# A four-step graph network kernel: type sums in short instructions, extra rows moved ahead, messages before scans

## The reference

```
def step(feat, _):
    transformed = jnp.einsum('nd,khd->knh', feat, W) + b[:, None, :]   # 4 edge types
    msgs = transformed[etypes, src]
    a = jax.ops.segment_sum(msgs, dst, num_segments=num_nodes)
    feat = _gru_cell(a, feat, w_ih, w_hh, b_ih, b_hh)
...
seg_sum = jax.ops.segment_sum(edge_attr, row, num_segments=N)
seg_max = jax.ops.segment_max(edge_attr, row, num_segments=N)
```

## Time and profile before

| | us |
|---|---|
| median of 3 runs | 7,605.77 (7,584.76 to 7,704.37) |
| the profiled execution | 7,588.8, span 7,587.1 |
| PE busy | 4,931.1 (65%) |
| VectorE, ScalarE, GpSimd busy | 4,188.5, 4,037.2, 3,838.4 |
| step 0, first product to end of contraction | 1,036.8 to 3,053.2 |
| step 1, first product | 3,102.4 |
| end of step 3's contraction, about | 5,890 |

### The profile page before, as it was taken

The page is one execution under the profiler, slowest core; times in us unless marked ns, Lnnn a source line. Parts: engine busy times, 40 slices in busy tenths (PEclk is TensorE's granted clock), DMA queues, the critical chain, the costliest instruction groups (busy, mean ns, idle before and its releaser), DMA issues. The chain is left out here.

```text
span 7587.1 us, 95171 instructions
## 1 busy us (share of the span) xinstructions
PE 4931.1 (65%) x39275; PEld 2509.5 (33%) x39275; DVE 4188.5 (55%) x6700; ACT 4037.2 (53%) x3030; POOL 3838.4 (51%) x3297
## 2 busy tenths in 40 slices
PE   0120135655544443899998999889999467666678
PEld 0110123332222221455554555545555311111123
DVE  9889953333322222455544555445554499999700
ACT  0000048888655654566664666646656177777501
POOL 0027778888877771577772677726771000000130
PEclk9955567877777776999998999999999666676799
DMA  9920035555433337466664776646666143333398
GB/s 414 429 41 0 0 115 200 199 196 198 150 134 139 140 139 134 160 229 235 207 219 139 232 242 214 213 143 229 237 217 203 36 163 149 153 153 153 130 417 361
DMA packets 344776, 1414.97 MB, mean 186 GB/s; under 512 B 129310, under 2 KB 182836, under 8 KB 314516
## 3 DMA queue, kind: packets, MB, share of 16 engines
q1 hardware_dynamic: 159676, 1138.67, 40.8%
q10 hardware_dynamic: 79672, 239.96, 8.8%
q0 software_dynamic: 104992, 30.24, 3.2%
HBM read 1008.21 MB, written 400.36 MB: 186 GB/s over the span
## 5 line engine op out<-in xcount | busy, mean ns | idle before, releaser
L556 PE MATMUL ps_all<-ring,T 128*64 128x448 f16 x32928 | 3323.2, 364 | 1069.9 <-ACT ring L713 1051.2
L556 PEld LDWEIGHTS ps_all<-ring,T 128*64 128x64 bf16 x32928 | 1902.7, 113 | 2472.2 <-ACT ring L713 789.8
L407 POOL DMA_INDIRECT mat_d<-cT,idxT x1563 | 1866.6, 1194 | 965.5 <-ACT cT L654 489.7
L451 POOL DMA_INDIRECT R<-in_edge_attr,eid x1568 | 1793.4, 1144 | 694.4 <-issue 477.2
L712 ACT ACTIVATE ring<-ring 128x3136 uint16<-128x3136 uint8 x504 | 1415.3, 2808 | 1330.2 <-DVE t L1047 823.5
L713 ACT ACTIVATE ring<-ring 128x3136 uint16<-128x3136 uint8 x504 | 1411.4, 2800 | 0.0
L1071 DVE TENSOR_TENSOR R<-ring 128x6272 uint16<-128x6272 uint16 x49 | 168.2, 3433 | 1363.5 <-ACT ring L713 1363.5
L1624 POOL DMA_INDIRECT sg<-seg_d,endI x49 | 56.9, 1161 | 1206.6 <-POOLq L178 1192.0
L510 PE MATMUL ps_all<-ident,R 128*128 128x128 f32 x448 | 109.7, 426 | 807.1 <-DVE R L807 807.1
L1567 PE MATMUL ps_all<-ad,ones 3*128 3x384 bf16 (+1 forms) x686 | 322.5, 470 | 337.1 <-ACT ps_all L1537 336.2
L1036 DVE TENSOR_SCALAR ring<-ring 128x3136 uint16<-128x3136 uint16 x308 | 303.7, 986 | 390.4 <-PE ps_all L556 265.0
(11 more groups left out here) (373 smaller groups left out, 3913.1 us busy)
## 6 DMA issues: line engine op xcount, KB each, us to landing
ring<-mat_d SPq DMA_DIRECT2D x784, 784.0 KB
C<-csum_d SPq DMA_DIRECT2D x98, 3136.0 KB, 15.3
mat_d<-ring SPq DMA_DIRECT2D x98, 1568.0 KB, 39.7
csum_d<-R ACTq DMA_DIRECT2D x196, 784.0 KB, 3.7
seg_d<-R ACTq DMA_DIRECT2D x32, 1568.0 KB
msg_d<-t ACTq DMA_DIRECT2D x196, 128.0 KB
R<-in_edge_attr,eid POOLq DMA_INDIRECT x1568
mat_d<-cT,idxT POOLq DMA_INDIRECT x1563
```

What stands on the lines that cost most here:

```text
L407: pool.indirect_dma_start(mat_d, bass.IndirectOffsetOnAxis(idxT[:, col:col + 1], 0), cT[:, col:col + 1], None).then_inc(s_sc[g % 8], 16)
L451: pool.indirect_dma_start(slab[n % 2][:, c, 0:FA], None, attr, bass.IndirectOffsetOnAxis(eid[:, at:at + 1], 0)).then_inc(s_at[n % 2], 16)
L556: mm = pe.matmul(accs[h * D:(h + 1) * D, j, 0:GW], lhsT, ring[:, n % 6, h * HQ + j * GW:h * HQ + (j + 1) * GW], start=first, stop=True, sk ...
```

## The change

It does four things. (1) `added` sums in 16 instructions instead of 3: two rounds of four uint16 adds over quarters, then eight `scalar_tensor_tensor` of 784 elements that add the fourth piece, write fp32 into the store buffers and give row sums; ScalarE only issues the stores. (2) All 49 messages of step 0 are made and stored once before step 0 (`early`), by products into PSUM banks 0 and 1; step 0 makes them again for its own use. (3) The extra rows' scatters and the gathers of their messages stand inside the stream of scatters, behind the 673rd, and their pieces are contracted before step 0's last block (`walk`); pieces from the extra rows on are widened by both engines. (4) In steps 1 to 3 VectorE makes the message and widens before it scans; a slab is scanned in three blocks instead of four, and GpSimd gathers the extra rows' messages ahead of a slab's gathers.

```diff
+EXTRA_GROUP = 42
+EXTRA_BLOCK = 42
...
+def walk(st):
+    return list(range(BPS)) if st else [*range(NB - 1), NB, NB + 1, NB - 1]
...
-        who = "act" if n < KT * NB or n % 2 else "dve"
+        who = "act" if n < KT * (NB - 1) or n % 2 else "dve"
...
+            psE = [bank(k)[:, 0:KT * D] for k in range(2)]
+            sumW = QW // 2
...
+                    if k == EXTRA_GROUP * GC:
+                        extra_placed()
+                        gathered(0)
...
-                pool.wait_ge(s_xs, 16 * NSG)
...
+                    if n and n % PER == 0 and n // PER < STEPS - 1:
+                        gathered(n // PER)
                     for c in range(SLAB):
                         at = n * SLAB + c
                         pool.indirect_dma_start(slab[n % 2][:, c, 0:FA], None, attr,
                                                 bass.IndirectOffsetOnAxis(eid[:, at:at + 1], 0)).then_inc(s_at[n % 2], 16)
-                    if n and n % PER == 0 and n // PER < STEPS - 1:
-                        gathered(n // PER)
...
+                for c in range(NB):
+                    if c >= 2:
+                        pe.wait_ge(s_tc, c - 1)
+                    product(c, psE[c % 2])
+                pe.wait_ge(s_tc, NB)
...
                     for o in range(NQ):
-                        n = c * NQ + o
-                        if n >= 2:
-                            act.wait_ge(s_cso[o % 2], 16 * (n // 2))
-                        act.activation(CS[o % 2], all4[:, o * QW:(o + 1) * QW], ACT.Copy,
-                                       accum_out=rs[:, c % 2, o:o + 1]).then_inc(s_cse, 1)
-                        act.wait_ge(s_cse, n + 1)
+                        act.wait_ge(s_csm, c * NQ + o + 1)
                         act.dma_start(csum[c * P:(c + 1) * P, o * QW:(o + 1) * QW], CS[o % 2]).then_inc(s_cso[o % 2], 16)
...
+                for c in range(NB):
+                    msgs_out(0, c)
                 for st in range(STEPS):
...
+                    for q in quarters:
+                        ad = dve.tensor_tensor(all4[:, q], four[0][:, q], four[1][:, q], ALU.add)
+                    link(ad)
+                    widened(dve, piece_no(0, c, 2))
+                    for q in quarters:
+                        ad = dve.tensor_tensor(all4[:, q], all4[:, q], four[2][:, q], ALU.add)
+                    link(ad)
+                    widened(dve, piece_no(0, c, 3))
+                    for o in range(NQ):
+                        n = c * NQ + o
+                        if n >= 2:
+                            dve.wait_ge(s_cso[o % 2], 16 * (n // 2))
+                        for h in range(2):
+                            at = slice(o * QW + h * sumW, o * QW + (h + 1) * sumW)
+                            ad = dve.scalar_tensor_tensor(CS[o % 2][:, h * sumW:(h + 1) * sumW], all4[:, at], 1.0, four[3][:, at],
+                                                          ALU.mult, ALU.add, accum_out=rs[:, 2 * o + h:2 * o + h + 1])
+                        ad.then_inc(s_csm, 1)
+                    dve.wait_ge(s_csm, (c + 1) * NQ)
+                    dve.tensor_reduce(cn_src[:, c:c + 1], rs[:, :], AX.X, ALU.add).then_inc(s_csr, 1)
...
-                    for f in range(q * FA // 4, (q + 1) * FA // 4):
+                    for f in range(q * FA // 3, (q + 1) * FA // 3):
...
-                        upto(piece_no(st, c, 0) + 5)
-                        if slab_of(st, c) is not None:
-                            scanned(*slab_of(st, c))
+                        upto(min(piece_no(st, c, 0) + 5, end))
                         if c + 2 < NB:
                             message(st, c + 2)
-                        elif c + 1 == NB:
+                        if c == (NB - 1 if st else EXTRA_BLOCK):
                             message_extra(st)
-                        upto(piece_no(st, c, 0) + 7)
...
+                        upto(min(piece_no(st, c, 0) + 7, end))
+                        if slab_of(st, c) is not None and slab_of(st, c)[1] < 3:
+                            scanned(*slab_of(st, c))
```

More of the change, by code:

```diff
@@ L68, with first_pieces, piece_no @@
 assert NS * SLAB == EC and HQ == NG * GW and NQ * QW == NP and SPEC * P + D == HQ and KT < NX <= 2 * KT
-def piece_no(st, c, k):
-    return PPS * st + KT * c + k
 def pieces(c):
     return KT if c <= NB else NX - KT
+def walk(st):
+    return list(range(BPS)) if st else [*range(NB - 1), NB, NB + 1, NB - 1]
+def first_pieces():
+    found = []
+    for st in range(STEPS):
+        n = PPS * st
+        for c in walk(st):
+            found.append(((st, c), n))
+            n += pieces(c)
+    return dict(found)
+FIRST_OF = first_pieces()
+def piece_no(st, c, k):
+    return FIRST_OF[st, c] + k
 def widened_by():
@@ L479, in _ @@
                 for st in range(STEPS):
-                    for c in range(BPS):
+                    for c in walk(st):
                         if st == 0 and c < NB:
@@ L605, in _ @@
                         pe.wait_ge(s_h, NG * st)
-                    product(st, 0)
-                    pe.wait_ge(s_tc, NB * st + 1)
-                    product(st, 1)
-                    for c in range(NB):
-                        contract(st, c)
-                    for c in range(NB, BPS):
-                        contract_extra(st, c)
+                    product(0, psT)
+                    pe.wait_ge(s_tc, NB * (st + 1) + 1)
+                    product(1, psT)
+                    for c in walk(st):
+                        if c < NB:
+                            contract(st, c)
+                        else:
+                            contract_extra(st, c)
                     gates(st)
@@ L759, in grown @@
                         act.activation(nn[j % 2], tt[j % 2], ACT.Tanh, bias=gb[:, 2:3]).then_inc(s_tn, 1)
+                for c in range(NB):
+                    msgs_out(0, c)
                 for st in range(STEPS):
+                    end = PPS * (st + 1) - 1
                     upto(piece_no(st, 0, 0))
-                    msgs_out(st, 0)
+                    if st:
+                        msgs_out(st, 0)
                     upto(piece_no(st, 0, KT - 1))
-                    msgs_out(st, 1)
-                    for c in range(NB):
-                        upto(piece_no(st, c, 0) + 5)
-                        if st == 0:
+                    if st:
+                        msgs_out(st, 1)
+                    for c in walk(st):
+                        upto(min(piece_no(st, c, 0) + 5, end))
+                        if st == 0 and c < NB:
                             sums_out(c)
@@ L1067, in added @@
                     four = [ring[:, piece_no(0, c, k) % 6, :].bitcast(U16) for k in range(KT)]
-                    widened(dve, piece_no(0, c, KT - 1))
-                    if c:
-                        dve.wait_ge(s_cse, c * NQ)
-                    link(dve.tensor_tensor(all4, four[0], four[1], ALU.add))
-                    link(dve.tensor_tensor(all4, all4, four[2], ALU.add))
-                    dve.tensor_tensor(all4, all4, four[3], ALU.add).then_inc(s_csm, 1)
-                def rows_summed(c):
-                    dve.wait_ge(s_cse, (c + 1) * NQ)
-                    own = rs[:, c % 2, :]
-                    link(dve.tensor_tensor(own[:, 4:6], own[:, 0:2], own[:, 2:4], ALU.add))
-                    dve.tensor_tensor(cn_src[:, c:c + 1], own[:, 4:5], own[:, 5:6], ALU.add).then_inc(s_csr, 1)
+                    quarters = [slice(o * QW, (o + 1) * QW) for o in range(NQ)]
@@ new lines, in added @@
+                    widened(dve, piece_no(0, c, 0))
+                    widened(dve, piece_no(0, c, 1))
+                    for q in quarters:
[6 more added lines that the diff above has]
+                    widened(dve, piece_no(0, c, 3))
@@ L1152, in grown @@
                         after(j)
+                for c in range(NB):
+                    early(c)
                 for st in range(STEPS):
+                    end = PPS * (st + 1) - 1
                     upto(piece_no(st, 0, 0))
```

86 lines of the change are left out of this document (43 added, 43 removed).

## The result

The changed kernel takes 7,344 us (median of four runs, 7,334 to 7,461), the kernel before 7,597 beside it; the ratio is 0.967, with a 95% interval of 0.966 to 0.969. One of the four runs took some 120 us more than the rest, as single runs of most kernels here did, and such runs are left out of all ratios. The forecast was 7,330. Its profiled execution takes 7,338.5 us (span 7,336.8), that of before 7,588.8: 250 less, where the prediction's sum said 268. The sum was nearly right, but two of its terms were not: step 0 gave more than it was to give, and steps 1 to 3 lost time instead of gaining.

What follows compares the result with a forecast made beforehand. Step 0 was taken as bound by GpSimd's scatters and a serial tail, steps 1 to 3 by nearly full PE. −186 − 40 − 42 = −268 on 7,588.8 gave 7,321, stated as 7,330 us; range 7,210 to 7,480.

Steps and rivals of the forecast that it cites:

- Sums in short instructions: Step 0's sums: 4.6 us of scatter time lost a block instead of 7.0, gain 110 us; last scatter at 2,767.
- its period is rounded up to whole VectorE instructions: Step 0's sums: a scatter enters at a boundary, every two instructions, 1.86 us; 8.1 scatters in a block's 15.0 us.
- The upper bound: Step 0's sums: loss grows with time held, 10.2 us a block, a loss of 147; as rival 7,578 us, chance 0.07.
- Extra rows: Step 0: eight scatters and seven gathers behind the 673rd scatter, at 1,456 us, add 19 us to the stream.
- rival 2: Step 0, mid-stream: the extra rows' DMA jam stops GpSimd, 80 us more before the last scatter, 7,410 us; chance 0.12.
- the jam: Step 0: DMA stands some 80 us from about 1,475 for the extra rows; PE loses it and makes it up.
- Early messages: Before step 0: 49 products, 60 us, first piece widened at about 1,103; costs nothing, or 60 to 159 without cover.
- Tail: Step 0's end: contraction ends about 100 us after the last scatter instead of 195, at 2,867, 186 earlier than before.
- Messages' gathers: Steps 1 and 2: gathers ahead of slab 11's 49 remove 40.3 us of PE's waits for T3e.
- Piece waits: Steps 1 to 3: 14 us a step, 42 in all, of PE's 79.5 us waiting for widened pieces go; between 0 and 79.5.
- Rate and number of scans stay: Steps 1 to 3: the new order with messages before scans leaves the scans' rate and number unchanged.
- The new deadline: Steps 1 to 3: behind a late slab, the next thing PE lacks comes 11 us later.

Runs made afterwards that it cites:

- the control: The changed kernel with one assertion on register values taken away; 7,333.8 us, ratio 0.968 to the kernel before.
- d4_act_late: Against the control, 40 unused ScalarE copies (about 60 us) between the early messages' stores and step 0's first widening; 7,359.2 us, ratio 0.9705.
- c1_long_adds: Against the control, the eight quarter adds made two whole uint16 adds again, the eight fp32-writing instructions kept; 7,510.1 us, ratio 0.991.
- d3_gather_behind: Against the control, the seven gathers of the extra rows' messages put behind slab 11's (22's) 49 gathers again; 7,422.1 us, ratio 0.980.
- c7_old_scans_gaps: Against the control, four scan portions ahead of the message, VectorE waiting after each portion's fourth pair; 9,493 us on a troubled chip (kernel before 10,341).

## Why the prediction was right, and where not

**Sums in short instructions.** Taken: 4.6 us lost a block, from the step "its period is rounded up to whole VectorE instructions: two of 0.91 to 0.97, 1.86 us". The period was rounded up to two, 1.77 us, and 7.8 scatters a block are caught (8.1 said). The size was off, as a caught scatter loses 0.44 us on the mean, and others pass free between: 3.46 us a block. (The recorded sum is also a little off: 3.8 scatters fewer at 1.265 us are 4.8 us, not 4.6.) 1.14 × 47 = 54 us, and the control's last scatter is 54 us ahead of the 2,767 predicted. The upper bound (the loss goes with the time held) is refuted by the long adds. A scatter beside an add is held for what is left of it, as the rows show. That adds of 1.23 us don't slow a scatter, as the prediction reads in the earlier trace rows, rests on one that started 0.04 us before its add, and isn't shown. The Trainium skill (SBUF — State Buffer, Who interferes with whom) says, of the modes in which VectorE takes the port pair that it shares with GpSimd, that the other side is blocked for the whole instruction; for the adds the trace agrees (held until 0.8 us after the add's end), but a run of scans and the widenings behind it held gathers far longer than any one instruction, up to 5.6 us.

**Extra rows.** GpSimd was not stopped (rival 2), the jam took some 40 us of PE's time (24 busy in 64) and these were made up, as the tail shows, which is no longer than forecast. The eight were issued from 1,443 on (1,456 said).

**Early messages.** First widening at 1,090 (1,103 said), nothing lost that the profile shows; no run took them away alone, d4_act_late only made the same delay longer.

**Tail.** 89 us instead of 100. The sums' leaving ScalarE, which the prediction put at nothing in itself, is part of it: with the sums of before the tail is 19 us longer. Together with the scatters the contraction ended 267 us earlier (251 in the control), not 186.

**Messages' gathers.** −40 said, −40 came in the waits; put back they cost 88.

**Piece waits.** Here the prediction failed: −42 said, +47 measured. The step that failed is "Rate and number of scans stay". The number stayed; the rate of the gathers did not (a slab every 75 to 79 us instead of 72 to 76), because the prediction priced the order of the scans only by what VectorE does later, and neither the length of their runs nor what now stands directly behind them. The trace of before held gathers of up to 3.18 us beside 16 scans, which could have been put to use: six scans more are 1.3 us more for a gather that is caught, and the two widenings that the new order puts behind the scans are 1.8 more. The new deadline, 11 us later, may have come; but slabs 5 us later each eat it in two slabs. Steps 1 to 3 as a whole were to give 82 us and took 15 more: 89 of the difference are these waits, the rest isn't traced. The two errors, −65 to −81 in step 0 and +97 in the steps, nearly cancel, and that the forecast of 7,330 met 7,344 is in part luck.

## What to carry to other kernels

Where VectorE and GpSimd run side by side, don't count VectorE's busy time but the longest stretch in which GpSimd can't get in: cut long two-input instructions into pieces shorter than GpSimd's own period, and break runs of very short ones by a wait of 0.1 us. A gap that costs VectorE 7 waits a slab gave 145 us here. When a loop is cut into fewer, longer portions, or moved, price the length of the unbroken run, with the instructions that follow it at once, even where number and place of the instructions seem to be all that changes.

## What the runs showed of the hardware

- A run of 16 scans, 0.215 us apart, makes a gather take up to 3.18 us; one of 22 with a wait behind it up to 3.84; one of 20 to 22 with two widenings directly behind it up to 5.6 (6.2 once in the control); at most eight with a gap of 0.12 us behind them up to 2.66, mostly 0.95. The held gather ends 0.8 us after the last instruction of the unbroken run. More than half of the gathers that start within a run of scans aren't held at all; what decides is in part how far into the run they start.
- The same can be much longer. In three of the fourteen profiles, of c1_long_adds, d3_gather_behind and c7_old_scans_gaps (this one on the troubled chip), one scatter beside the second sort stood for 136.9 us, while VectorE issued over 250 instructions one after the other, 0.33 to 0.85 us apart. It ended 0.8 us after VectorE's first pause of 0.11 us. The executions of the first two took 138 and 116 us more than the median of their kernels' runs. First that of c1_long_adds, then the same place in the changed kernel, where the scatters got in:

```profile
569.66 136.88 POOL L447 DMA_INDIRECT mat_d<-cT,idxT  x1 [0.30 <-issue]
570.00 0.59 DVE L848 SCALAR_TENSOR_TENSOR R<-R 128x256 f32<-128x256 f32 x1
```

```profile
573.22 1.24 POOL L447 DMA_INDIRECT mat_d<-cT,idxT  x1 [0.30 <-issue]
573.54 0.60 DVE L849 SCALAR_TENSOR_TENSOR R<-R 128x256 f32<-128x256 f32 x1
```

  Same instructions, same order, and the same phase to some hundredths of a us (the scatter starts 0.18 us into an instruction of VectorE here, 0.20 there); what decides isn't shown. Because of this hold the last scatter of c1_long_adds in its profile (3,014) is not used above.
- A reduction, with its single input, doesn't hold GpSimd, where an instruction with two inputs of the same length does. Timeline of c1_long_adds: beside a reduction of 3,136 elements (3.42 us) the scatters take 0.96, beside the two-input instruction behind it 3.98:

```profile
521.28 3.42 DVE L234 TENSOR_REDUCE m<-ring 128x49 f32<-128x3136 f32 x1 [0.58 <-DVE i_place L1012]
522.92 0.96 POOL L447 DMA_INDIRECT mat_d<-cT,idxT  x1 [0.31 <-issue]
...
525.17 3.43 DVE L236 TENSOR_TENSOR ring<-ring,m 128x3136 f32<-128x3136 f32 x1
525.45 3.98 POOL L447 DMA_INDIRECT mat_d<-cT,idxT  x1 [0.30 <-issue]
```

  The Trainium skill (SBUF — State Buffer, Who interferes with whom) says that a reduction never contends on this chip; by that rule the trace agrees. A single input is not enough, though: the widenings have one each, and hold gathers as shown above.
- Eight scatters of the extra rows keep DMA engines busy at 0.95 while 101 GB/s are moved, for some 60 us, and this jam moves with them from kernel to kernel. Why they do it, and the matrix's scatters of one-byte rows don't, isn't shown.
